# Cross attention in rounds of two steps, with four score banks and context blocks loaded in place

## The reference, cut to what matters

```python
q = (query @ Wq + bq).reshape(b, s, 16, 64)
k = (key @ Wk + bk).reshape(b, key.shape[1], 16, 64)
v = (value @ Wv + bv).reshape(b, value.shape[1], 16, 64)
logits = einsum('bshd,bShd->bhsS', q, k) / sqrt(64)
attn = einsum('bhsS,bShd->bshd', softmax(logits), v).reshape(b, s, 1024)
return attn @ Wo + bo

x = x + xattn(layernorm(x), ctx, ctx)      # the above
x = x + attn(layernorm(x))                 # 16 heads of 32 over the 128 rows of a batch
x = x + ffn(layernorm(x))                  # gated q, k, v of 16 experts, causal attention, gated o_proj
```

## Time and profile before

| | |
|---|---|
| median of 3 runs | 1403.63 us |
| the profiled execution | 1407.57 us, span 1405.8 us |
| TensorE busy | 1360.4 us, 97% |
| DVE, ACT, POOL busy | 882.1, 503.4, 179.3 us |
| mean granted TensorE clock | 0.985 |
| HBM traffic | 69.53 MB read, 52 GB/s over the span |

### The profile page before, as it was taken

How to read it: one execution, slowest core, us unless ns; L and a number is a source line. 1 busy time by engine, 2 the same in 40 slices (tenths; PEclk the granted TensorE clock), 3 DMA queues, 4 the chain that set the end, 5 groups by cost and what they waited for, 6 DMA issues and landing times.

```text
span 1405.8 us, 22386 instructions
## 1 busy us (share of the span) xinstructions
PE 1360.4 (97%) x9196; PEld 1099.6 (78%) x9196; DVE 882.1 (63%) x1280; ACT 503.4 (36%) x686; POOL 179.3 (13%) x140
## 2 busy tenths in 40 slices
PE   6999999999999999999999999999999987899999
PEld 5877888778878887887888778878887875688877
DVE  6426763695457448843763596357647467788779
ACT  4226541473135216520641363135314544311210
POOL 2211100140010004200100150010000500000030
PEclk9999999999999999999999999999999997799999
DMA  7400100240020004201100150011001321014200
GB/s 224 139 23 27 42 10 10 68 132 10 10 70 10 10 10 138 71 1 40 41 19 10 46 153 11 10 54 27 10 10 54 98 92 61 32 60 138 91 12 31
DMA packets 41107, 74.11 MB, mean 53 GB/s; under 512 B 6608, under 2 KB 10720, under 8 KB 39984
## 3 DMA queue, kind: packets, MB, share of 16 engines
q1 hardware_dynamic: 40096, 70.28, 16.1%
q0 software_dynamic: 912, 2.41, 0.5%
HBM read 69.53 MB, written 3.15 MB: 52 GB/s over the span
## 4 chain that ended last, share of the span: by engine, by line
PE 85%; DVE 10%; issue 2%; ACT 1%; DMA 1%; POOL 0%; SPq 0%; DVEq 0%; ACTq 0%
PE b_ps L1163 26%; PE b_ps L1185 21%; PE b_ps L476 9%; PE b_ps L1200 8%; PE b_ps L1235 7%; PE b_ps L399 3%; PE b_ps L502 3%; PE b_ps L1173 2%; DVE b_prob L1494 2%; PE b_ps L1261 2%; DVE b_mx L1476 2%; DVE b_sm L1503 1%; DVE b_ctxT L1392 1%; PE b_ps L1215 1%; DMA stage<-in_ctx 1%
## 5 line engine op out<-in xcount | busy, mean ns | idle before, releaser
L1185 PE MATMUL b_ps<-b_ctxT,wk 128*128 128x512 f32 x1536 | 389.8, 402 | 0.6 <-issue 0.6
L1163 PE MATMUL b_ps<-wv,b_ctxT 128*128 128x512 f32 x1536 | 368.8, 398 | 12.1 <-DVE b_ctxT L1392 12.0
L1163 PEld LDWEIGHTS b_ps<-wv,b_ctxT 128*128 128x128 f32 x1536 | 287.5, 189 | 83.2 <-issue 14.9
L1185 PEld LDWEIGHTS b_ps<-b_ctxT,wk 128*128 128x128 f32 x1536 | 281.5, 188 | 76.1 <-issue 11.2
L1363 ACT ACTIVATE b_kst<-b_ps,b_bkT 128x512 f32<-128x512 f32 x128 | 88.0, 688 | 460.9 <-PE b_ps L1185 459.7
L1410 DVE COPY b_V<-b_ps 128x512 f32<-128x512 f32 x128 | 88.4, 691 | 215.4 <-PE b_ps L1163 215.4
L1494 DVE TENSOR_TENSOR b_prob<-b_prob,b_ps 128x2048 f32<-128x2048 f32 x64 | 145.9, 2281 | 51.5 <-PE b_ps L1215 51.5
L1200 PEld LDWEIGHTS b_ps<-b_q,b_kst 64*128 64x128 f32 x2048 | 125.1, 188 | 40.0 <-issue 36.3
L1200 PE MATMUL b_ps<-b_q,b_kst 64*128 64x128 f32 x2048 | 149.5, 285 | 7.0 <-DVE b_mx L1476 7.0
L1373 ACT COPY b_prob<-b_ps 128x1024 f32<-128x1024 f32 x128 | 129.8, 1014 | 72.0 <-PE b_ps L1200 71.4
L1235 PE MATMUL b_ps<-b_prob,b_V 128*64 128x128 f32 x2048 | 138.1, 277 | 0.0
(11 more groups left out here) (206 smaller groups left out, 1216.3 us busy)
## 6 DMA issues: line engine op xcount, KB each, us to landing
stage<-in_ctx SPq DMA_DIRECT2D x64, 256.0 KB, 3.0
b_wo<-in_Wo SPq DMA_DIRECT2D x8, 1024.0 KB, 5.1
stage<-in_Wk SPq DMA_DIRECT2D x30, 256.0 KB, 2.7
stage<-in_Wv SPq DMA_DIRECT2D x28, 256.0 KB, 3.1
stage<-in_self_w SPq DMA_DIRECT2D x16, 256.0 KB, 2.8
t_raw<-in_q_proj SPq DMA_DIRECT2D x16, 256.0 KB, 4.2
t_raw<-in_k_proj SPq DMA_DIRECT2D x16, 256.0 KB, 3.5
t_raw<-in_v_proj SPq DMA_DIRECT2D x16, 256.0 KB, 3.7
```

Of the source, the lines that this page charges most:

```text
L1163: mm = nc.tensor.matmul(ps[:, G.bank[item]], ctxT[:, a, k, n * P:(n + 1) * P], wv[:, w, k], start=m == 0, stop=m == len(terms) - 1)
L1185: mm = nc.tensor.matmul(ps[:, G.bank["k", t]], wk[:, i % 2, w, k], ctxT[:, a, k, s * BANK:(s + 1) * BANK], start=m == 0, stop=m == len(ter ...
```

## The change

1. **Rounds.** The loops go over rounds of two steps. A round is: both key products; in even rounds `turn_top`; both scores products, for the same two steps and not the one before; in even rounds `spread_top`; `weigh` of two steps, four rounds behind; then the items of both steps.
2. **Four score banks.** Scores of even steps go to banks 2 and 3, of odd steps to 4 and 5. The ring for keys, values and output products shrinks from four banks to two (0 and 1).
3. **ACT and DVE lists** follow: the exponents of a pair run in an odd round, each ahead of a key copy; DVE does two `max_step` in the even round and all sums in the odd one. Value products lie as 6, 6 and 4 chunks in three rounds, not 4 in each of four steps.
4. **Context in place.** A block of 1 MB (four chunks) is loaded straight into the place of the low part of `ctxT` (`ctx_raw`), once the last keys and values have read it; the low part then overwrites it. The staging slots are left to the weights. Of the first context, four chunks come one by one in pieces of 512 bytes.
5. **Drain and tail.** The steps past the last (the drain) are 128 to 135, not 128 to 137; the logits of batch 0 (`sl00` to `sl03`) and part of their normalising move into it; the string `TAIL` is reordered.

The diff, cut to its core:

```diff
-    LAG_WEIGH, RING = 8, 4
+    LAG_WEIGH, RING, SCORE_BANKS = 4, 2, (2, 3, 4, 5)
-                self.products[half * h + 7 + n // SB].append(("v", h, n))
+                self.products[half * h + 4 + 2 * (n // 6)].append(("v", h, n))
-        work += [(self.STEPS * b - (4 if b < NB else 3) + n // 2 - n // 6, ("ctx", b, n)) for b in ... for n in range(NC)]
+        for b in range(1, NB + 1):
+            for n, t in enumerate(CHUNK_STEPS):   # (-3, -3, -2, -2, -1, -1, -1, -1, 0, 0, 0, 0, 1, 1, 1, 1)
+                self.splits[self.STEPS * b + t].append(("ctx", b, n))
+        ctx_raw = at("ctx_raw", [P, C, S], ctx_at + 4 * C * S)
+            def load_chunk(b, n):
+                if b > 0:
+                    sp.wait_ge(k_psum, STEPS * b - SB + n // SB + 1)
+                    sp.wait_ge(v_psum, NC * (2 * b - 1) + n + SB)
...
+                    sp.dma_start(ctx_raw[:, :, n * P:n * P + BANK], src).then_inc(block_in[n // SB], 16)
-                if t > 0:
-                    pe.wait_ge(s_out, t)
-                    pe.wait_ge(top_done, (SB - 1) * ((t - 1) // SB) + (t - 1) % SB)
+                if t < 2:
+                    pe.wait_ge(v_out, NC)
+                else:
+                    pe.wait_ge(s_out, t - 1)
+                    pe.wait_ge(top_done, (SB - 1) * ((t - 2) // SB) + (t - 2) % SB)
# PE
+            for r in range(G.ROUNDS):
+                if 2 * r < TOTAL:
+                    for t in steps:
+                        keys(t)
+                if 0 <= complete < NB * NP:
+                    turn_top(complete)
+                if 2 * r < TOTAL:
+                    for t in steps:
+                        scores(t)
+                if 2 * r < TOTAL and complete >= 0:
+                    spread_top(complete)
+                if unit >= 0:
+                    weigh(2 * unit)
+                    weigh(2 * unit + 1)
# ACT
+                for t in (2 * r, 2 * r + 1):
+                    if r % 2 == 1 and 0 <= r - 3 < 2 * NB * NP:
+                        exponent(r - 3 + t % 2)
+                    if t < TOTAL:
+                        key_out(t)
+                    if t % 2 == 0:
+                        for item in G.splits[t]:
+                            split_hi(item)
+                if 2 * r < TOTAL:
+                    scores_out(2 * r)
+                    scores_out(2 * r + 1)
# DVE
+                if r % 2 == 0:
+                    if i - 1 in pairs:
+                        max_step(i - 1, 2)
+                        max_step(i - 1, 3)
+                        max_end(i - 1)
+                    chunks_rest(2 * r)
+                    if i - 3 in summed:
+                        attention_out(i - 3)
+                    if i - 1 in pairs:
+                        max_rows(i - 1)
+                        below_max(i - 1, 0)
+                        below_max(i - 1, 1)
+                else:
+                    if i in pairs:
+                        max_step(i, 1)
+                    chunks_rest(2 * r)
+                    if i - 1 in summed:
+                        for s in range(1, SB):
+                            sum_step(i - 1, s)
+                        sum_end(i - 1)
+                chunks_rest(2 * r + 1)
# tables
-              127: "xl2 sx2", 128: "pq0", 129: "pq1 pq2 pq3", 132: "pk0 pk1", 133: "const", 134: "pk2", 135: "pk3",
+              126: "xl2 sx2", 127: "pq0 pq1", 128: "pk0", 129: "pk1 pk2 pq2", 130: "pk3 pq3",
+              131: "xf0 sl00 sl01 sl02 sl03", 132: "sv0", 133: "sr00 sr01 sr02", 135: "sv1 const sr03"}
```

260 lines of the change are left out of this document (116 added, 144 removed).

## The result

The changed kernel takes **1412.24 us** (median of five, 1410.85 to 1415.13), the kernel before 1404.17 us (1402.61 to 1407.92) on the same chip: a ratio of 1.0058, interval 1.0040 to 1.0075. It is slower by 0.6%; the forecast was 1384 us, faster by 1.4%.

The account below looks back on a forecast made before the run. TensorE's own list was taken to bound the kernel (busy 1360.4 of 1405.8 us). 1407.6 - 19.5 + 3.1 - 3 = 1388.2, less 3.9 for the runs' median, gave 1384 us; range 1366 to 1400, the forecast's own 1376 to 1393.

Parts of the forecast that it names:

- Part 1, TensorE's own time: Steps in pairs: fewer changes of matmul tiling, about 0.2 us a border, save 0.61 us a pair, -19.5 us over 32.
- Part 2, the 1 MB load in place taken as hidden: Context loads: issued when the last keys have read the block, cast most of a 10 us round later, so no cost.
- Part 2, the other new waits at a boundary: Three context boundaries: two casts +0.9, DVE's low parts +1.2, chunks ahead of the row maximum +0.3; 2.4 each, +7.2 us.
- Part 2, waits in the seven rounds with a value weight (+2.8): Odd rounds: the value weight's cast on ACT delays the second key copy by 0.4 us, in seven rounds, +2.8 us.
- 6.9 us of old waits: Steps before the drain: the scores' waits for the running maximum go with two pairs of score banks, -6.9 us.
- The ring of two banks costs nothing: Value products: each takes 2.81 us and its copy is due one product later, so two banks suffice; 0 us.
- Part 3, the drain: Drain and what follows: 9.3 us of old waits and clock loss against 6.5 of new waits, -3 us net.
- the wait for the last normalisation: Behind the last output product: the last normalisation's transposes wait 2.3 us and a little more for their copy, 2.5 us.
- Part 4, the tail: Rest of the tail, 1164 to 1230 us: same chain members in another order, none removed; 0, ends -14 and +8.
- the tail gives too: Rival: earlier logits of batch 0 remove half of the 30 us lost in the tail, 14 us, 1370 us; chance 0.18.
- The load in place comes late: Rival: context blocks land 5 us later than assumed, two exposed at each of three boundaries, +15, 1399 us; chance 0.09.
- The side "slower": Whole kernel slower than 1410.6 us: the case of ACT's list bounding odd rounds and a little more; chance 0.08.

Follow-up runs that it names:

- e9: e1 with the first weighing block of each round put between the two score blocks, same products: 1422.64 us.
- e1: The changed kernel with the four block loads of a new context ahead of wo and the staged weights in SyncE's list: 1395.28 us.
- e7: The changed kernel with only block 0 of a new context ahead of the weights in SyncE's list, blocks 1 to 3 unmoved: 1398.65 us.
- e14: e1 with two drain items moved and, at boundaries, VectorE's row maxima first, sums' last step later, eleven lower parts on VectorE, GpSimd held back: 1382.39 us.
- e16: e14 without the two lines that hold GpSimd back before its lower parts of chunks 13 to 15: 1393.80 us.
- e15: e1 with only two drain items moved (ln0 to step 119, ln2 behind the transposes of step 123): 1395.16 us.

## Why the prediction was wrong, by its own steps

- **Part 1, TensorE's own time: right in size, not in all places.** Forecast 0.61 us a pair, measured 0.56 in the clean pair and 9.4 us over the 17 undisturbed pairs, 0.55 each; e9 gives 0.17 us for a border where the forecast had 0.2. In the first four pairs it does not show, since keys(0) to keys(16) take 74.0 us in both kernels: TensorE has 52 more records ahead of keys(16) now (one block of scores, two of weighting and their sums), some 3.1 us by the earlier trace rows (an estimate), which it has no more in the drain. Six pairs lie at boundaries and five in the drain, where other things set the time.
- **Part 2, the 1 MB load in place taken as hidden: this is the step that failed.** It said that the load "is issued when the last keys have read the block". It is issued when SyncE's list comes to it. I never walked that list, which a step that moves into a queue asks for: `wo` and two weights stand ahead of block 0, a weight load that waits for a slot ahead of blocks 1 to 3. I named the place on which the wait would fall, ScalarE and through the key copy TensorE, and there it fell, and at keys(33), the longest wait of all, on GpSimd's lower parts. The step cost 16.3 us at three boundaries (e1); with block 0 alone ahead 13.9 of them come back (e7). Part of that is the half clock around the waits, which this part of the forecast did not allow for.
- **Part 2, the other new waits at a boundary: too small.** I charged 2.4 us each. With the gain of the two pairs there, and the waits of before that were to go (4.4 us at three boundaries), a boundary was to be 0.3 us shorter than before; with the loads out of the way it is 2.9, 2.9 and 1.8 us longer (e1). The causes that I gave (ScalarE's two casts, VectorE's order) left one out: VectorE's work with both operands in SBUF takes about twice as long beside GpSimd. With order, split and GpSimd's start mended, the boundaries are 0.7, 0.7 and 1.8 us shorter than before (e14), 3.6 us each of it by GpSimd's start alone (e16); how much of e1's own loss is that and how much is order was not tested apart.
- **Part 2, waits in the seven rounds with a value weight (+2.8): they never came.** No scores product in these rounds waits for a key copy. Of the 6.9 us of old waits that I took from the earlier trace rows, 4.4 lay at the boundaries, 1.8 in the first four pairs and 0.7 in the undisturbed steps; they did go, but new waits of the transposes for the running maximum came (3.3 us in five).
- **"The ring of two banks costs nothing": not quite.** The keys of step 124 wait 1.24 us for the residual addition of an output product, since VectorE stands at a normalisation ahead of it. What it costs in the end can't be told (e15).
- **Part 3, the drain: the wait for the last normalisation was right** (2.5 forecast, 2.62 us measured at 1158.14), and the wait for the first normalised probabilities is gone. Of the other two waits of the forecast, that of the first projection is 1.77 us (2.5 forecast) and that of the logits 0.17 (1.5 forecast); 1.33 and 1.24 us of waits ahead of them were not foreseen. From keys(108) to the last output product the changed kernel takes 2.4 us more; 4.2 us of work moved in from behind and 3.1 us moved out to the start.
- **Part 4, the tail: 0 was wrong.** From the last output product to the end it is 261.3 instead of 271.6 us. I gave "the tail gives too" 0.18 with 14 us; it gave about 10, 4 of them moved from behind the last output product to ahead of it.
- **The sum.** Forecast -19.4, measured +7.3 between the spans: 26.7 us apart. With each forecast term put where its waits lie, the boundaries are 24.7 of them (forecast 7.2 - 4.4 - 6 x 0.61 = -0.8, measured +23.9), the start 4.6 (-3.9 against +0.7, with 3.1 of work moved there), the undisturbed steps -0.7 (-8.7 against -9.4), drain and tail together -1.9 (-6.0 against -7.9). Of the 24.7, e1 gives 16.3 back. With the queue set right the span is 1392.9 (e1), with VectorE and GpSimd kept apart 1378.8 (e14), on either side of the forecast's span, 1405.8 - 19.4 = 1386.4.
- **The rivals.** "The load in place comes late" (0.09) was the true one. Its size was too small: it took a block to be 5 us late and priced that at 1399. It is the issue that was late, by up to 12.6 us; from issue to landing a block takes 6.0 us in e1 and 9.1 in the changed kernel, where three go together (medians at the first boundary). The side "slower" had 0.08.

## What to carry to other kernels

When a transfer moves into an engine's queue, write out that queue around it, with what each entry ahead of it waits for; an entry that waits for a buffer holds all that stands behind it, and its buffer may wait for the very transfer. Put transfers whose place comes free by the main engine ahead of those that wait for staging. Where GpSimd takes work off VectorE, place it beside VectorE's work on PSUM, even by holding it back: here the same work 3 us earlier, at three places, cost 11 us.

## What the runs showed of the hardware that I had not expected

- VectorE beside GpSimd: five lower parts (both operands in SBUF, 128x512) 3.09 us alone, 7.41 beside three of GpSimd; two sums 2.56 and 4.39; the last sum 0.43 and 1.37. With an operand in PSUM: 2.28 and 2.28, 1.22 and 1.22. GpSimd's own go from 1.28 to as much as 1.86.
- Around TensorE's wait of 3.83 us the granted clock fell to 0.50 for 6.8 us, so a wait is paid again in part: twelve key products behind it take 5.46 us instead of 3.04. In the changed kernel 17 us at 0.50 lie at the three boundaries, in e1 none.
- A border between row-split and column-split products costs 0.17 us within "busy" (e9), much like one with full products (0.56 / 3 = 0.19 us in the clean pair).
